# A two-layer attention and expert kernel on one core: experts by halves of the batch, fp32 products in the last network, exps read from PSUM, and a new order of the work

## The chip, the cores and the metric

One core of one Trainium2 chip runs the kernel. The metric is the device time of one execution in microseconds (us). Three runs of the kernel before gave a median of 160.07 us (159.89 to 160.13).

## What is computed

Eight sequences of 128 tokens with 128 features go through four blocks, each added to its own input. Cut to what matters:

```python
x = x + softmax(LN(x) @ ctx.T) @ ctx                      # first attention, 77 context rows per sequence
m = heads(LN(x)) @ o_w + o_b                              # 16 heads over 128 tokens
x = LN(x) + x + 0.3 * sum_e comb[e] * (gelu(m @ w1[e] + b1[e]) @ w2[e] + b2[e])   # 8 experts, 2 weights not zero
Sim = hc @ w1s + (hq @ w2s) + (hc * w3) @ hq.T + b_sim    # hc = LN(x), hq = ctx: second attention
A = softmax(Sim, 2); B = softmax(max(Sim, 2), 1)
hat = A @ hq; bar = B @ hc
x = x + [hc, hat, hc * hat, hc * bar] @ W_qv + b_qv
h = gelu(LN(x) @ W1[7] + b1[7])                           # last network, one expert of hidden size 512
x = x + (h @ W2[7] + b2[7]) * softmax(LN(x) @ Wr.T)[7]
```

The term `hq @ w2s` is one number for each row of the context: the context's row, the same for all tokens.

## The kernel before

**Queues.** The order of the work is one list written out by hand, `plan`. Each engine's program walks it and runs the stages that it owns, so the list fixes the order on PE, ACT, DVE, POOL and SP at once; semaphores join the queues. A stage is named with its arguments: `m1:u,e,c` is the first product of expert e for the tokens of unit u and half c of the hidden features, `gelu:u,e` its two gelus on ACT, `m2:u,e` its second product, `acc:u,e` the weighted adds on DVE. PE never reorders.

**Units.** From the experts on, the batch goes in three units: unit 0 is sequences 0 to 3 (512 tokens), units 1 and 2 are two sequences each (256 tokens). In the kernel before every stage of the experts is done for each unit. `m1` is two products in fp32r (low part of w1 and high part, each against the tokens, line 1098, which is a helper through which nearly all products go), 512 or 256 columns wide; `m2` is in fp32, 128 columns, which the profile shows as two records for each product: 16 records for a unit of four sequences, 8 for a unit of two. `h1_bank` names the PSUM banks of m1: two pairs of banks, taken in turn.

**Second attention** (`p4_*`), for each unit: layer norm (`p4_ln`, the power on POOL at line 571, `p4_norm`), transposes to x3T (`p4_T`), the similarities (`p4_sim`), on DVE an add of `simrow` (line 1006), the maximum and its subtraction (line 1011), one exp over the unit's scores (`p4_exp`, line 727, ACT), the softmax over the tokens through `p4_mx`, `p4_nbm` and `bex` (line 730), the sums and the scaling (`p4_probs`), transposes (`p4_pT`), products with context and tokens (`p4_hq`), `p4_hh` on DVE, the output products (`p4_out`, 3 for each sequence) and `p4_outd` on DVE (line 1048). `simrow` holds the context's row for all sequences; PE makes it in two products 308 wide between the heads (`p4_ctx`, with `w2sq`), ACT copies it (line 718).

**Last network** (`p5_*`): layer norm, transposes (`p5_T`), router (8 columns), `p5_f1:u,c` as three fp32r products (`split3`; ACT makes the high part of the tokens at line 751, DVE the low part at line 1058), a gelu each (line 760), `p5_f2:u,i` in fp32 for each sequence, the last add on DVE (line 1084) and the store. `p5_exp:2`, `p5_prob:2` and `p5_end:2` come after the last gelus.

ACT holds one set of function tables: exp and ln are in one set, gelu in another, and each change of set is an ACT_TABLE_LOAD. `warm` and `hot` are products with no use for the result, which keep PE busy.

## Time and profile before

| what | before |
|---|---|
| median of 3 runs | 160.07 us |
| the profiled execution, its own time | 160.33 us |
| its span on the core | 158.5 us |
| PE busy with products | 146.0 us (92%) |
| PE loading weights | 118.0 us (74%) |
| DVE, ACT, POOL busy | 109.3, 105.9, 50.5 us |
| stages in time | front to 30, heads to 71, experts from 71, second attention and last network among them from 103 |

The span is the time from the first to the last instruction; 1.8 us of the execution lie around it. Busy shares are averages over stages, and the ends of PE's records are modelled: successive products overlap in the record. What a product costs in a stream is the distance from its start to the next start, and a wait of PE is where that distance exceeds the usual one of its kind.

### The profile page before, as it was taken

Reading aid. Unit: us, or ns where it says so; the run is one execution under the profiler, and the core shown is the slowest. Engines: PE = TensorE matmul, PEld = TensorE weight load, DVE = VectorE, ACT = ScalarE, POOL = GpSimd, SP = SyncE. Lnnn points to the kernel's source line nnn. Section 1 sums busy time; section 2 is a strip of 40 time slices with the busy share of each in tenths; the row PEclk is TensorE's granted clock in tenths of the full one; section 3 lists DMA queues with packets and bytes.
Section 4 is the critical chain, followed back from the end, with each engine's and each line's share of the span. In section 5 each row is a group of like instructions: output and inputs, shape, how many; then the busy total and the mean of one; then the engine's idle time right before and its main releaser. Section 6 shows DMA issues by size and latency. Waiting matters only on the chain.

```text
span 158.5 us, 3986 instructions
## 1 busy us (share of the span) xinstructions
PE 146.0 (92%) x1288; PEld 118.0 (74%) x1296; DVE 109.3 (69%) x413; ACT 105.9 (67%) x238; POOL 50.5 (32%) x155
## 2 busy tenths in 40 slices
PE   7898995889999999999999999998999999999891
PEld 5676872555766557567998999997899889779780
DVE  3666999978877749832269656963764968687733
ACT  5697795368388677999489344657941894666480
POOL 7799500234244478594000001400430200400100
PEclk9999999999999999999999999999999999999999
DMA  3528700743557423100100000000000000000022
GB/s 100 156 76 271 203 2 0 149 115 74 113 155 181 104 50 54 19 2 4 35 0 4 0 0 0 4 0 2 0 4 0 2 6 0 0 0 2 4 67 65
DMA packets 11072, 8.03 MB, mean 51 GB/s; under 512 B 1867, under 2 KB 10155, under 8 KB 11051
## 3 DMA queue, kind: packets, MB, share of 16 engines
q1 hardware_dynamic: 11051, 7.76, 19.7%
q8 instruction: 11, 0.18, 0.5%
q14 instruction: 10, 0.08, 0.2%
HBM read 5.26 MB, written 1.70 MB: 44 GB/s over the span
## 4 chain that ended last, share of the span: by engine, by line
PE 49%; issue 21%; DVE 14%; ACT 7%; POOL 4%; DMA 2%; ACTq 1%; SPq 1%; POOLq 1%; DVEq 0%
PE ps L1098 47%; DVE qbd L876 2%; DVE nmax L882 2%; DMA x<-in_x_dram 2%; POOL rstd L571 2%; DVE stats L784 1%; DVE xn L799 1%; ACT pr L631 1%; ACT pexp L662 1%; POOL xn L565 1%; ACTq L58 1%; ACT L727 1%; DVE mv L788 1%; ACT mT L655 1%; DVE res L851 1%
## 5 line engine op out<-in xcount | busy, mean ns | idle before, releaser
L712 ACT ACTIVATE vpad<-ps,b1o 128x256 f32<-128x256 f32 (+1 forms) x48 | 23.3, 543 | 17.3 <-PE ps L1098 17.1
L1098 PE MATMUL ps<-w2s,vpad 128*128 128x128 f32 x256 | 32.4, 276 | 0.0
L1098 PEld LDWEIGHTS ps<-w2s,vpad 128*128 128x128 f32 x256 | 30.4, 192 | 0.8 <-issue 0.2
L995 DVE SCALAR_TENSOR_TENSOR vpad<-ps,comb,vpad 128x128 f32<-128x128 f32 x64 | 18.4, 343 | 10.3 <-PE ps L1098 10.1
L882 DVE TENSOR_REDUCE nmax<-ps 128x4 f32<-128x512 f32 x32 | 20.9, 685 | 5.5 <-PE ps L1098 5.4
L662 ACT ACTIVATE pexp<-ps 128x512 f32<-128x512 f32 x32 | 18.2, 594 | 2.5 <-PE ps L1098 1.9
L1098 PE MATMUL ps<-ao,w_lo 128*128 128x256 f32 (+1 forms) x48 | 16.4, 356 | 0.8 <-ACT vpad L712 0.8
L1098 PE MATMUL ps<-ao,w_hi 128*128 128x256 f32 (+1 forms) x48 | 14.6, 318 | 0.0
L565 POOL TENSOR_TENSOR xn<-vpad,bqv 128x256 f32<-128x256 f32 (+1 forms) x3 | 2.7, 915 | 36.5 <-DVE vpad L995 36.5
L571 POOL TENSOR_TENSOR rstd<-veps,power 128x2 f32<-128x2 f32 (+1 forms) x6 | 4.8, 808 | 28.2 <-DVE veps L794 28.2
L1098 PE MATMUL ps<-kst,qbd 128*128 128x128 bf16 x128 | 11.8, 219 | 2.1 <-DVE nmax L882 2.1
L1098 PEld LDWEIGHTS ps<-kst,qbd 128*128 128x128 bf16 x128 | 8.6, 97 | 6.8 <-issue 5.0
L1098 PE MATMUL ps<-qbd,kst 128*128 128x512 bf16 x32 | 12.1, 383 | 0.9 <-ACT mT L655 0.3
L1098 PE MATMUL ps<-pexp,vpad 128*32 128x128 f32 x256 | 10.8, 280 | 0.2
L1098 PEld LDWEIGHTS ps<-ao,w_lo 128*128 128x128 f32 x48 | 9.1, 189 | 2.5 <-issue 1.8
L1098 PE MATMUL ps<-ones 128*128 128x256 bf16 x46 | 9.3, 336 | 1.1 <-DVE pair L775 1.1
L1098 PEld LDWEIGHTS ps<-ao,w_hi 128*128 128x128 f32 x48 | 9.1, 189 | 0.4
L556 POOL COPY qbd<-mT 3x256 f32<-3x256 f32 x16 | 6.6, 414 | 7.7 <-ACT mT L655 7.3
L760 ACT ACTIVATE qbd<-ps,cols 128x256 f32<-128x256 f32 (+1 forms) x12 | 6.3, 544 | 3.8 <-PE ps L1098 3.7
L1098 PEld LDWEIGHTS ps<-pexp,vpad 128*32 128x32 f32 x256 | 5.9, 108 | 3.5 <-issue 1.3
L1098 PE MATMUL ps<-f2s,qbd 128*128 128x128 f32 x64 | 8.3, 278 | 0.0
L541 POOL CAST xn<-nmax 128x16 bf16<-128x16 f32 x8 | 2.0, 255 | 19.0 <-DVE nmax L882 18.9
(228 smaller groups left out, 331.2 us busy)
## 6 DMA issues: line engine op xcount, KB each, us to landing
w1s<-in_L_ffn_w_dram SPq DMA_DIRECT2D x1, 1024.0 KB, 5.4
kst<-scratch_k SPq DMA_DIRECT2D x8, 72.0 KB
qbd<-scratch_q SPq DMA_DIRECT2D x8, 72.0 KB
w1s<-w1s SPq DMA_DIRECT2D x8, 64.0 KB
x<-in_x_dram SPq DMA_DIRECT2D x2, 192.0 KB, 3.6
scratch_q<-part SPq DMA_DIRECT2D x2, 144.0 KB, 2.6
scratch_k<-part SPq DMA_DIRECT2D x2, 144.0 KB, 2.5
wqv<-in_L_xattn_W_qv_dram SPq DMA_DIRECT2D x1, 256.0 KB, 3.2
```

The lines of the kernel that those rows point to most:

```text
L58: with stack:
L541: a = did(pool.tensor_copy(m[:, :, 0, :], v))
L556: last = pool.tensor_copy(qbd[r, g, :, b * S:(b + 1) * S].bitcast(FP32), mT[r, b % 2, :, :].bitcast(FP32))
L565: pool.tensor_tensor(out=x2b[:, seqs(u), :], in0=x2[:, seqs(u), :], in1=bqv[:, :].unsqueeze(1).to_broadcast([P, UNITS[u][1], D]), op=ALU.a ...
L571: pool.tensor_tensor(out=rstd[:, i, seqs(u)], in0=veps[:, i, seqs(u)], in1=power[:, seqs(u)], op=ALU.pow).then_inc(s[f"ln{i}_rstd"], 1)
L662: act.activation(pexp[:, n % 3, :], ps[:, 2 + n % 2, :], ACT.Exp, scale=KPH ** -0.5).then_inc(s["p_ok"], 1)
L712: act.activation(hT[:, k % 2, c, 0:n], ps[:, h1_bank(k, c), 0:n], ACT.Gelu, bias=b1o[:, e, c:c + 1]).then_inc(s["gelu_ok"], 1)
L760: act.activation(gT[:, c, toks(u)], ps[:, (bank_a, bank_b)[c % 2][u], 0:UNITS[u][1] * S], ACT.Gelu, bias=cols[:, R_FB1 + c:R_FB1 + c + 1]) ...
L876: last = dve.tensor_scalar(out=qbd[r, g, j, 0:FRONT[0][1] * S], in0=kst[r, g, T // 2:T], scalar1=used1[r, 0:1], scalar2=None, op0=ALU.mult)
L882: dve.tensor_reduce(nmax[:, b, g, :], ps[:, n % 2, :].rearrange("p (j t) -> p j t", t=S), axis=AX.X, op=ALU.max, negate=True).then_inc(s[" ...
L995: dve.scalar_tensor_tensor(out=x2[:, a + i, :], in0=ps[:, 2 + k % 2, i * D:(i + 1) * D], scalar=comb[:, a + i, e:e + 1], in1=x2[:, a + i, ...
L1098: return nc.tensor.matmul(dst, lhsT, rhs, start=start, stop=stop)
```

## The change

Five parts. (1) `m1` and `gelu` run for two halves of the batch instead of three units: half 1 holds units 1 and 2, all products are 512 wide; the gelus of half 1 go to a buffer of their own for all eight experts (`hT1`, in the room of the dead `qbd`), so they wait for no `m2`; `m2` and `acc` stay by units. The last network's gelus move to other dead tiles. (2) `p5_f1` of units 1 and 2 is one fp32 product instead of three fp32r ones; ACT's copy of the high part and DVE's subtraction fall away there. (3) The context's row is added by PE in `p4_sim` itself, as a product that accumulates in the same bank; `p4_ctx`, `simrow` and the add on DVE go. DVE takes the negated maximum from PSUM; the exps are taken from PSUM for each sequence with that maximum as bias and an accumulated sum (2 or 4 instead of 1), so DVE's subtraction and sum go too; a small DVE operation makes `nmb`, from which the softmax over the tokens is made. (4) In `p4_out` of units 1 and 2 the two products that don't need `hh` come first, each sequence in a bank of its own. (5) The whole `plan` is in a new order. There are 43 `warm` products instead of 44 and one `hot` instead of two; before the first transposes of the context stand 12 `warm` instead of 20. By SP's queue nothing changes: the same transfers in the same order. On ACT the changes of table fall from ten to eight after the first load: `p4_exp:0` and `p4_exp:1` now stand with no gelu between them.

The diff, cut to its core (of the plan: the front's part that the text speaks of, and everything from `p4_T:0` on):

```diff
-            p1_soft:1 p1_pT:1 warm:2 p1_ln:0 warm:1 z_den warm:1 spare warm:1 p1_norm1:0 setup p1_av:1 a_q:2 p1_T2:0 p1_T:2 warm:1
...
-            av:6,3 s2:7,2 av:7,0 fb s2:7,3 p4_ctx:1 norm:5 den:6 av:7,1 av:7,2 un:7 x2_init:0 norm:6 av:7,3 cT:0 den:7 m1:0,0,0
...
-            m1:1,4,0 m1:1,4,1 x2b:1 m1:1,5,0 m1:1,5,1 m2:1,3 acc:1,2 p4_T:0 m2:1,4 gelu:1,5 p4_norm:0 gelu:1,6 p4_sim:0 m1:1,6,0
-            m1:1,6,1 m1:1,7,0 acc:1,3 m2:1,5 m1:1,7,1 m1:2,0,0 acc:1,4 m2:1,6 p4_simd:0 m1:2,0,1 acc:1,5 gelu:1,7 m1:2,1,0 acc:1,6
-            p4_mx:0 m2:1,7 p4_nbm:0 gelu:2,0 p4_exp:0 gelu:2,1 p4_probs:0 m2:2,0 m1:2,1,1 acc:1,7 p4_pT:0 gelu:2,2 m1:2,2,0
-            m1:2,2,1 acc:2,0 fw1 p4_ln:1 m2:2,1 p4_hq:0 p4_norm:1 m1:2,3,0 m1:2,3,1 m2:2,2 p4_hh:0 acc:2,1 m1:2,4,0 m1:2,4,1
-            gelu:2,3 acc:2,2 gelu:2,4 p4_outd:0 gelu:2,5 p4_T:1 p5_ln:0 acc:2,3 p4_out:0 m2:2,3 m1:2,5,0 acc:2,4 gelu:2,6
-            p4_simd:1 m1:2,5,1 m2:2,4 acc:2,5 p4_exp:1 gelu:2,7 p4_nbm:1 p5_norm:0 m1:2,6,0 m1:2,6,1 p4_sim:1 m2:2,5 p4_probs:1
-            p4_mx:1 m1:2,7,0 m1:2,7,1 p5_T:0 m2:2,6 acc:2,6 acc:2,7 p4_pT:1 m2:2,7 p5_router:0 p4_hh:1 p4_ln:2 p4_hq:1 p5_f1:0,0
-            p4_norm:2 p5_f1:0,1 p4_outd:1 p4_out:1 p5_f1:0,2 p4_T:2 p5_ln:1 p5_f1:0,3 p4_sim:2 p4_simd:2 x2b:2 p5_norm:1 p5_exp:0
-            p4_nbm:2 p5_f2:0,0 p4_mx:2 p4_exp:2 p4_probs:2 p5_f2:0,1 p5_prob:0 p4_pT:2 p5_T:1 p4_hq:2 p4_hh:2 p5_f2:0,2
-            p5_router:1 p4_outd:2 p5_exp:1 p4_out:2 p5_f1:1,0 p5_ln:2 p5_norm:2 p5_f1:1,1 p5_f2:0,3 p5_f1:1,2 p5_f1:1,3 p5_T:2
-            p5_prob:1 p5_f2:1,0 p5_router:2 p5_end:0 p5_end:1 p5_f1:2,0 p5_prob:2 p5_f1:2,1 p5_f1:2,2 p5_f1:2,3 p5_f2:1,1
-            p5_f2:2,0 p5_f2:2,1 p5_end:2 p5_exp:2
...
+            p1_pT:1 warm:4 p1_ln:0 a_q:1 warm:1 spare p1_norm1:0 warm:2 p1_av:1 setup p1_T2:0 oT warm:2 p1_qk:0 p1_ln:1 p1_split:0
...
+            norm:5 av:7,1 av:7,2 s2:7,3 den:6 norm:6 av:7,3 un:7 cT:0 den:7 norm:7 m1:0,0,0 x2_init:0 gelu:0,0 b2:0 gelu:0,1
...
+            gelu:1,4 acc:1,3 gelu:1,5 p4_T:0 m1:1,5,1 m1:1,6,0 acc:1,4 m1:1,6,1 m2:1,3 m2:1,4 gelu:1,6 m1:1,7,0 gelu:1,7 x2b:0
+            m1:1,7,1 m2:1,5 p4_sim:0 m2:1,6 p4_mx:0 m2:1,7 p4_exp:0 acc:1,5 p4_simd:0 m2:2,0 acc:1,6 p4_pT:0 p4_nbm:0 p4_probs:0
+            x2b:1 acc:1,7 p4_hq:0 m2:2,1 m2:2,2 acc:2,0 da:1 p4_hh:0 acc:2,1 p4_ln:1 acc:2,2 p4_norm:1 p4_out:0 p4_outd:0 p4_T:1
+            p5_ln:0 acc:2,3 p4_simd:1 x2b:2 m2:2,3 p5_norm:0 p4_exp:1 p4_sim:1 acc:2,4 acc:2,5 p4_nbm:1 m2:2,4 p4_probs:1 p4_mx:1
+            acc:2,6 m2:2,5 acc:2,7 p5_T:0 m2:2,6 m2:2,7 p4_pT:1 p5_router:0 p4_hq:1 p4_hh:1 p5_f1:0,0 p5_f1:0,1 p4_out:1 p4_ln:2
+            p5_f1:0,2 p4_norm:2 p4_T:2 p5_f1:0,3 p4_exp:2 p4_sim:2 p4_mx:2 p4_outd:1 p5_ln:1 p5_f2:0,0 p4_simd:2 p4_nbm:2
+            p5_norm:1 p5_f2:0,1 p4_pT:2 p5_exp:0 p5_T:1 p4_hq:2 p4_probs:2 p4_hh:2 p5_router:1 p5_exp:1 p4_outd:2 p5_ln:2
+            p5_f2:0,2 p4_out:2 p5_f1:1,0 p5_f1:1,1 p5_f1:1,2 p5_f1:1,3 p5_f2:0,3 p5_norm:2 p5_T:2 p5_f2:1,0 p5_prob:0 p5_router:2
+            p5_f1:2,0 p5_f1:2,1 p5_prob:1 p5_f1:2,2 p5_end:0 p5_end:1 p5_f1:2,3 p5_prob:2 p5_end:2 p5_f2:1,1 p5_f2:2,0 p5_exp:2
+            p5_f2:2,1
...
                 for c in range(F0):
                     act.wait_ge(s["h1_ps"], F0 * k + c + 1)
-                    if k >= 2:
+                    if u == 0 and k >= 2:
                         act.wait_ge(s["h2_ps"], k - 1)
                     if k == 0:
                         act.wait_ge(s["b1o_ok"], 1)
-                    act.activation(hT[:, k % 2, c, 0:n], ps[:, h1_bank(k, c), 0:n], ACT.Gelu,
+                    act.activation(hT1[:, e, c, :] if u else hT[:, k % 2, c, :], ps[:, h1_bank(k, c), :], ACT.Gelu,
                                    bias=b1o[:, e, c:c + 1]).then_inc(s["gelu_ok"], 1)
-
...
+                    act.activation(pr[1][:, b, :], ps[:, bank_b[u], m * CTX:(m + 1) * CTX], ACT.Exp, bias=mx[1][:, b:b + 1],
+                                   accum_out=rs[1][:, b:b + 1]).then_inc(s["pr1_ok"], 1)
                 act.wait_ge(s["nbm_ok"], u + 1)
-                act.activation(bex[0:n, u, :], ps[0:n, bank_b[u], 0:S], ACT.Exp, bias=nbm[0:n, u:u + 1],
+                act.activation(bex[0:n, u, :], ps[0:n, bank_a[u], 0:S], ACT.Exp, bias=nbm[0:n, u:u + 1], scale=-1.0,
                                accum_out=bsum[0:n, u:u + 1]).then_inc(s["bex_ok"], 1)
 
...
                 dve.wait_ge(s["sim_ps"], u + 1)
-                dve.wait_ge(s["sr_ok"], NHALF)
-                dve.tensor_tensor(out=sc[1][:, us, :], in0=ps[:, bank_b[u], 0:n * CTX].rearrange("p (b c) -> p b c", c=CTX),
-                                  in1=simrow[:, us, :], op=ALU.add).then_inc(s["sc1_ok"], 1)
-                dve.wait_ge(s["sc1_ok"], u + 1)
-                a = did(dve.tensor_reduce(mx[1][:, us], sc[1][:, us, :], axis=AX.X, op=ALU.max))
-                after(a)
-                dve.tensor_tensor(out=sc[1][:, us, :], in0=sc[1][:, us, :], in1=wide(mx[1][:, us])(CTX),
-                                  op=ALU.subtract).then_inc(s["sim_sub"], 1)
+                dve.tensor_reduce(mx[1][:, us], ps[:, bank_b[u], 0:n * CTX].rearrange("p (b c) -> p b c", c=CTX), axis=AX.X,
+                                  op=ALU.max, negate=True).then_inc(s["sim_max"], 1)
+                dve.wait_ge(s["sim_max"], u + 1)
...
-                    pe.wait_ge(s["gelu_ok"], F0 * (k - (2 if k <= 2 * E0 else 1)) + c + 1)
+                    pe.wait_ge(s["gelu_ok"], F0 * (k - 2) + c + 1)
                 f = slice(c * P, (c + 1) * P)
-                dst, x = ps[:, h1_bank(k, c), 0:n], ao2[:, :, :].rearrange("p h t -> p (h t)")[:, toks(u)]
+                dst, x = ps[:, h1_bank(k, c), :], ao2[:, u, :]
                 mm(dst, w1_lo[:, e, f], x, True, False)
...
+                pe.wait_ge(s["w2sq_ok"], 1)
+                pe.wait_ge(s["ctxT_ok"], NFRONT)
+                mm(ps[:, bank_b[u], 0:n * CTX], w2sq[:, :], ctxT[:, seqs(u), :].rearrange("p b c -> p (b c)"), True, False)
                 pe.wait_ge(s["xT2_ok"], u + 1)
                 pe.wait_ge(s["ctxw_ok"], NHALF)
                 for m in range(n):
-                    last = mm(ps[:, bank_b[u], m * CTX:(m + 1) * CTX], x3T[:, toks(u, m)], ctxw[:, a + m, :])
+                    last = mm(ps[:, bank_b[u], m * CTX:(m + 1) * CTX], x3T[:, toks(u, m)], ctxw[:, a + m, :], False, m == n - 1)
...
+                pe.wait_ge(s["w14_ok"], u + 1)
+                if u:
+                    for m in range(UNITS[u][1]):
+                        p4_two(u, m)
                 pe.wait_ge(s["hh_ok"], u + 1)
-                pe.wait_ge(s["w14_ok"], u + 1)
-                for m in range(n):
-                    dst = ps[:, bank_b[u], m * D:(m + 1) * D]
-                    mm(dst, hqT[:, toks(u, m)], wqv[:, 1, :], True, False)
-                    mm(dst, hhT[:, toks(u, m)], wqv[:, 2, :], False, False)
-                    last = mm(dst, x3T[:, toks(u, m)], w14[:, a + m, :], False, True)
+                for m in range(UNITS[u][1]):
+                    if u == 0:
+                        p4_two(u, m)
+                    last = mm(p4_bank(u, m), hhT[:, toks(u, m)], wqv[:, 2, :], False, True)
                 last.then_inc(s["qv_ps"], 1)
...
+                    pe.wait_ge(s["l7_sub"] if c else s["xT3_ok"] if u else s["x4hi_ok"], u + 1)
                 f = slice(c * P, (c + 1) * P)
-                split3(ps[:, (bank_a, bank_b)[c % 2][u], 0:UNITS[u][1] * S], f1_hi[:, f], f1_lo[:, f],
-                       x4_hi[:, toks(u)], x4_lo[:, toks(u)]).then_inc(s["f1_ps"], 1)
+                dst = ps[:, (bank_a, bank_b)[c % 2][u], 0:UNITS[u][1] * S]
+                if u == 0:
+                    last = split3(dst, f1_hi[:, f], f1_lo[:, f], x4_hi[:, toks(u)], x4_lo[:, toks(u)])
+                else:
+                    last = mm(dst, f1s[:, f], x4T[:, toks(u)])
+                last.then_inc(s["f1_ps"], 1)
 
...
```

## Rows read from the trace of the kernel before

**Rows 1.** Windows: length; busy us of PE, PEld, DVE, ACT, POOL; PEclk, DMA share, GB/s.
```profile
14.96:30.49 15.53, 12.78 (x92) 9.07 (x90) 15.01 (x53) 10.36 (x26) 4.29 (x11) 1.00 0.37 95
30.49:70.95 40.46, 38.74 (x493) 24.90 (x501) 29.98 (x86) 31.17 (x74) 21.93 (x76) 1.00 0.40 90
70.95:103.16 32.21, 32.21 (x247) 29.70 (x247) 19.62 (x87) 20.22 (x35) 4.57 (x6) 1.00 0.03 6
103.16:152.18 49.02, 46.85 (x362) 42.31 (x361) 34.25 (x138) 31.56 (x71) 7.02 (x9) 1.00 0.01 2
152.18:158.50 6.32, 2.84 (x26) 2.65 (x24) 2.07 (x8) 1.97 (x3) 0.00 (x0) 1.00 0.29 83
```

**Rows 2.** Timeline of PE, m1 512 wide: start us, us, then the instruction.
```profile
84.37 0.39 PE L1098 MATMUL ps<-ao,w_hi 128*128 128x512 f32 x1
...
87.40 0.43 PE L1098 MATMUL ps<-ao,w_lo 128*128 128x512 f32 x1
```

**Rows 3.** Timeline of PE, m1 256 wide, then m2 of 16 records.
```profile
98.52 0.37 PE L1098 MATMUL ps<-ao,w_lo 128*128 128x256 f32 x1
98.72 0.28 PE L1098 MATMUL ps<-ao,w_hi 128*128 128x256 f32 x1
...
99.54 1.95 PE L1098 MATMUL ps<-w2s,vpad 128*128 128x128 f32 x16
101.24 0.37 PE L1098 MATMUL ps<-ao,w_lo 128*128 128x256 f32 x1
```

**Rows 4.** Timeline of PE, f1 of unit 1 as three products.
```profile
144.97 0.36 PE L1098 MATMUL ps<-ao_hi,f_lo 128*128 128x256 f32 x1
...
145.76 1.05 PE L1098 MATMUL ps<-f2s,qbd 128*128 128x128 f32 x8
```

**Rows 5.** Timeline of PE, an fp32 product 512 wide (two records).
```profile
24.33 1.10 PE L1098 MATMUL ps<-w1s,woT 128*128 128x512 f32 x2 [0.33 <-ACT w1s L694]
25.27 0.49 PE L1161 MATMUL ps<-ident,pr 128*77 128x128 f32 x3
```

**Rows 6.** Timeline of PE, the second p4_ctx product and what follows it.
```profile
68.61 0.68 PE L1098 MATMUL ps<-ctxT,w2sq 128*128 128x308 f32 x2
69.13 0.38 PE L1098 MATMUL ps<-un,selden 128*128 128x128 f32 x2
```

**Rows 7.** Groups by line and shape: busy us, mean ns, idle before and releaser.
```profile
L712 ACT ACTIVATE vpad<-ps,b1o 128x256 f32<-128x256 f32 x32 | 13.4, 471 | 11.0 <-PE ps L1098 10.9
L712 ACT ACTIVATE vpad<-ps,b1o 128x512 f32<-128x512 f32 x16 | 9.9, 687 | 6.3 <-PE ps L1098 6.2
L718 ACT ACTIVATE simrow<-ps,bsim 128x308 f32<-128x308 f32 x2 | 1.0, 518 | 0.0
```

**Rows 8.** Timeline of ACT, a change of table and the exp behind it.
```profile
109.52 1.28 ACT L727 ACT_TABLE_LOAD   x1
110.81 0.46 ACT L727 ACTIVATE pr<-sc 128x308 f32<-128x308 f32 x1
```

**Rows 9.** Timeline of PE, a wait behind that stretch of ACT.
```profile
108.53 0.28 PE L1098 MATMUL ps<-ao,w_hi 128*128 128x256 f32 x1
109.28 0.36 PE L1098 MATMUL ps<-ao,w_lo 128*128 128x256 f32 x1 [0.48 <-ACT vpad L712]
```

**Rows 10.** Timeline of DVE, the add and the subtraction around the maximum of unit 0.
```profile
105.60 0.48 DVE L1006 TENSOR_TENSOR sc<-ps,simrow 128x308 f32<-128x308 f32 x1 [0.30 <-PE ps L1098]
...
106.62 0.48 DVE L1011 TENSOR_TENSOR sc<-sc,mx 128x308 f32<-128x308 f32 x1
```

**Rows 11.** Chain of waits: three exps with accumulated sums, first attention.
```profile
11.21 1.00 ACT pr L631 x6
```

**Rows 12.** Timelines of DVE and POOL behind p4_out of unit 0.
```profile
121.99 0.69 DVE L1048 TENSOR_TENSOR vpad<-ps,xn 128x512 f32<-128x512 f32 x1 [2.21 <-PE ps L1098]
...
124.28 1.01 POOL L571 TENSOR_TENSOR rstd<-veps,power 128x4 f32<-128x4 f32 x1 [7.84 <-DVE veps L794]
```

**Rows 13.** Timeline of PE in the front, the output products of the first attention.
```profile
13.99 0.94 PE L1098 MATMUL ps<-ctxn,pT 77*128 77x128 f32 x6
```

136 lines of the change are left out of this document (73 added, 63 removed).

## The prediction, made before the changed kernel ran

> **What bounds the kernel now.** I read the windows first, cut where the work changes: front, heads, first experts, everything from the first transposes of the second attention (`p4_T:0`, 103.16), and the end from the last f1 product (152.18) [rows 1]. The reader is to see that three regimes follow each other. From 14.96 to 30.49 DVE is busy 15.0 of 15.5 us: the front is DVE's. From 30.49 to 70.95 PE is busy 38.7 of 40.5 us. From 70.95 to 103.16 it is busy all the time: there only PE's own work counts. From 103.16 to 152.18 it shows 46.9 of 49.0, and DVE and ACT have room. The granted clock is 1.00 (2.4 GHz) in all of them. Next I read PE's timeline by distances from start to start, since the records overlap. m1 512 wide: thirteen steps from 84.37 to 87.40, 0.233 each [rows 2]. m1 256 wide: the first product behind another kind takes 0.20, the next seven fill 98.72 to 99.54, 0.117 each; m2's 16 records take 1.70, with their entry about 1.78, so 8 records 0.85 to 0.89 [rows 3]. With such prices the stretch from 103.16 to 152.18 holds 44.0 us of products: 12 m2 10.7, 20 m1 pairs 256 wide 5.7, `p4_out` 5.3, f1 6.5, five f2 4.5, sim, hq, transposes, routers and the rest 11.3. So **5.0 us of its 49.0 are waits of PE**, more than the busy share lets one think. Such a wait is the one behind ACT at 108.53 to 109.28: 0.75 from start to start where 0.12 is usual [rows 9].
>
> **The change part by part.**
>
> *Halves of the experts.* 64 products 256 wide (64 x 0.117 = 7.5, and some 16 entries of 0.08 more, 8.8) become 32 of 512 wide (32 x 0.233 = 7.5, some 7 entries, 8.0): 0.8 off PE. Twice the columns cost twice the time, so only entries are saved. On ACT a whole batch half is 32 gelus 256 wide or 16 gelus 512 wide: 13.4 busy against 9.9 [rows 7], 3.5 off, and nothing waits for it where PE is full. But the work moves: up to `p4_T:0` PE now runs 11 pairs 512 wide (5.5) where it ran 12 pairs 256 wide and one more m2 (3.2 + 0.9), so **the stretch from 70.95 gets 1.4 longer**, and the one after it loses 20 pairs (5.7), gains 5 (2.5) and that m2: 2.3 less.
>
> *fp32 in f1.* Three products in a stream are 0.40, half of the 0.79 that six take [rows 4]. An fp32 product 512 wide takes 0.94 [rows 5], half as wide 0.47: 8 x 0.07 = 0.6 more, 0.2 once the entries it saves are taken off. DVE and ACT lose about 0.4 each for two units; the last router no longer stands behind the subtraction. I take +0.2 in PE's work; bounds 0 and +0.6.
>
> *The context's row.* 0.52 for a product 308 wide [rows 6]; the two in the heads go (1.04), and 0.52 + 0.26 + 0.26 come into the later stretch. DVE's add and subtraction of 0.48 [rows 10] go: `p4_sim` to the exps is 1.0 shorter for unit 0, some 0.65 for the small ones. The exps get longer: three with sums took 1.00 [rows 11], so four take 1.3 and two 0.7 instead of 0.46 [rows 8] and about 0.3. Net 0.2 to 0.3 off the chain of each unit.
>
> *Tables.* In the row the exp starts 1.29 after the table's start [rows 8]: a change costs ACT 1.29, two fewer give 2.6. The Trainium skill, page "ScalarE: Activation LUTs", section "What ACT_TABLE_LOAD costs", counts 2.66 us for a change, as a drain follows the load. By it two changes fewer would give ACT 5.3; the row shows no such drain, so I stay with 1.29, and the rule is the ground of the third rival.
>
> *Heads and front.* `hot` once less, 0.1. Without `p4_ctx:1` the last exp of the heads has only `den:6` beside it: `av:7,3` waits for an exp (308 wide it is 0.46 [rows 8]) and its latency, with less than 0.3 of cover; I take 0.5 for that wait, between 0 and 0.8. So the heads get 1.04 + 0.1 - 0.5 = 0.65 shorter. In the front `p1_av:1`, which started at 13.99 [rows 13], behind the columns' transposes, now goes before them, about 0.7 earlier; DVE, which is full after it [rows 1], starts earlier but also meets ACT's fills before `rows:0`; I take 0.3 of the 0.7. The rest of the new order in front and heads can't be read from rows: PE is idle for 1.7 us in the heads and 2.7 in the front [rows 1], and the order may give back or cost 1.0. I take nothing, and keep -1.0 and +1.0.
>
> *The long stretch.* I went through the new list from `p4_T:0` (time 0), each stage at its price, each wait by its releaser:
> - PE's fillers (T, three m1, two m2, two m1, m2) and the row with sim:0 reach 7.0; maximum 0.5, four exps 1.3, bex and scaling 1.1 end at 9.8, PE comes to pT:0 at 10.0: covered. hq:0 ends at 12.4, two m2 14.2, out:0 16.9.
> - Behind out:0 DVE has the add and the statistics, 2.3 from 121.99 to POOL's start [rows 12], the acc of m2:2,3 and the maximum: 20.4. PE stands at mx:1 from 19.6: **wait 0.8**. Then m2:2,5, p5_T:0 (POOL's 1.0 is just covered), two m2, pT:1, router, hq:1: 26.2; two f1 27.6; out:1 29.0.
> - f1, T:2, f1, sim:2: 31.4. mx:2 waits 0.6. Two f2: 34.1. The gelu-to-exp change on ACT ends at 32.8, so pT:2 is just ready; hq:2 waits 0.3, out:2 ends at 38.5, four f1 (0.3 of waits), f2, T:2, f2 and the router at 42.8, the last f1 at 45.0.
>
> That is 45.0 against 49.0, with 2.1 us of waits instead of 5.0. What went: the m1 that waited for gelus behind the tables, of which one is shown [rows 9], and the waits before mx:1, pT:1 and T:2. What is late next is DVE behind out:0. Such a walk finds no collisions of two late queues; where half of the 2.9 us of recovered waits come back, the stretch is at 46.5. **I take 46.0, 3.0 less.** The end, 6.3 us from there [rows 1], is the same chain: gelu, table, exp, router's probabilities, add.
>
> **Sum:** front -0.3, heads -0.65, first experts +1.4, long stretch -3.0, order elsewhere 0: -2.55. The profiled execution's own time, 160.33 (span 158.5 and 1.8 around it), becomes 157.8; the median of the runs stands 0.26 below that execution, so I forecast **157.5**. A measurement can tell some 0.2% from no change, 0.3 us here.
>
> **The rivals.**
>
> *Only the work goes (chance 0.19).* PE's own work falls by 0.8 (m1) + 0.1 (hot) - 0.2 (f1), 0.7; if other waits take the place of the old, the time falls by 0.3 to 1.7: 158.4 to 159.8. For it: DVE is the late one in my walk already. Against it: DVE and ACT lose work in that very stretch.
>
> *The order is better everywhere (0.15).* If the walk holds in full (-4.0) and the order of heads and front gives back 1 of their 4.4 us of waits, it is -0.3 - 0.65 + 1.4 - 4.0 - 1.0 = -4.55, with more up to -6: 154 to 156. For it: ACT loses 3.5 of gelus, 2.6 of tables and the 1.0 of `simrow` [rows 7]. The rule of the Trainium skill on table changes (the page named above) points this way, but more strongly: with 1.4 more for each of the two changes that go, ACT would give back 2.8 more. As rows have it, PE waited 0.63 behind one such place [rows 9]; two places with 1.3 each would be the most, inside this rival.
>
> *Slower: the second attention runs out of cover (0.10).* Before, 20 m1 pairs (5.7 us) stood between the links of the chain norm, transposes, scores, exps, transposes, products, norm of units 0 and 1. Now only m2 stand there. If that chain and not PE sets the stretch, it stays at 49.0 or grows by the longer exps (0.9) while the first experts are 1.4 longer and heads and front 0.95 shorter: 160.1 + 0.5 to + 1.4, 160.6 to 161.5. It decides from 48.6 us of stretch. Against it: in the rows unit 0 needs 5.2 from the scores' add (105.60) to the exp (110.81) only since gelus and a table stood before it [rows 8, 10].
>
> *The front loses its clock or its DVE time (0.02).* All stretches show the granted clock at 1.00 [rows 1], but with 12 instead of 20 products before the first transposes PE does less there. At half the clock for some microseconds, or with DVE later, the price is an estimated 1 to 3.5: up to 161.
>
> *The change does nothing that counts (0.04):* within 0.3 of 160.07.
>
> **How the numbers follow.** The forecast's own case, -1.7 to -4.0, has 0.50: 156.1 to 158.4. Faster by over 0.2%: 0.50 + 0.19 + 0.15 = 0.84; within 0.2%: 0.05 with the edge of the slower case; slower: 0.11. The range: 156.1 to 158.4 holds 0.50; up to 159.8 takes in the second case; down to 155.3 takes half of the third (the walk in full, -4.55, is 155.5). Together about 0.78.
>
> **What would show it.** In the changed kernel: m1 starts 0.233 apart and 32 such products only; `p4_T:0` about 0.4 later than 103.16 (102 to 104); from it to the last f1 45 to 47; the first wait of PE there before the small `nmb` product of unit 1; nine tables in all; ACT's exps 0.33 apart; `av:7,3` behind the last exp. Wrong would be a stretch of 48.6 or more, a wait over 1 us before pT:0 or T:0 of the last network, DVE later than 15 in the front, or f1 fp32 products over 0.55 each.

## The result: 0.66% faster, where 1.6% was forecast

The changed kernel took 160.06 us (median of 20 runs, 158.73 to 161.16), the kernel before 160.91 in the 20 runs beside it (159.86 to 162.63). The medians differ by 0.85 us. The ratio, which leaves out the few runs that are far above the fastest of their kernel, is 0.9934, 95% interval 0.9908 to 0.9959, which of 160.91 is 1.06 us less. The sign was right; the forecast was 2.6 us less and 157.5, and the measured time lies outside the range. Part of the distance is the base: with the later runs the kernel before lies 0.8 above the 160.07 of its first three. Both kernels have runs in which TensorE is granted half its clock for some 3.4 us, and these take about 1 us more (e1 and e17 below). The runs of the changed kernel with a mean clock of 0.995 or more have a median of 159.2 (20 of the 32 taken, e3 included), those of the kernel before 160.3 (47 of the 122 with a clock on record). With the low clock it is 160.3 against 161.4. So the change is worth 1.1 us either way, over all runs; the two kernels with the fill of e1 and e2 differ by less, 0.6.

The page of the changed kernel, its span, its PE line and the granted clock in 40 slices:

```profile
span 158.2 us, 3846 instructions
PE 146.2 (92%) x1256; PEld 116.2 (73%) x1256; DVE 107.6 (68%) x405; ACT 100.7 (64%) x229; POOL 50.6 (32%) x155
PEclk9999999699999999999999999999999999999999
```

PE (TensorE) is as busy as it was; part of this execution ran at half the clock, and with the clock even (e1 and e2) it is 146.6 against 147.2. The windows of the changed kernel, cut at the same places as [rows 1] (`fold:0`, the first m1, `p4_T:0`, the last block of f2; columns as there):

```profile
22.62:71.15 48.53, 45.31 (x528) 27.59 (x528) 36.68 (x108) 33.44 (x82) 21.27 (x78) 0.96 0.36 83
71.15:104.80 33.65, 33.65 (x236) 30.11 (x236) 20.51 (x83) 22.64 (x36) 8.00 (x11) 1.00 0.02 5
104.80:151.84 47.04, 45.07 (x338) 40.57 (x337) 31.95 (x132) 24.69 (x63) 5.65 (x7) 1.00 0.01 2
151.84:158.20 6.36, 2.84 (x25) 2.65 (x23) 2.52 (x10) 1.97 (x3) 0.00 (x0) 1.00 0.31 85
```

Read against [rows 1]: the first experts 32.21 to 33.65, so 1.44 longer; the long stretch 49.02 to 47.04, 1.98 shorter; the end 6.32 to 6.36. The heads show a mean clock of 0.96, so this profile can't say what they gained; e1 and e2 can.

Waits of PE in the long stretch, timeline of the changed kernel (all with an idle time of 0.2 or more):

```profile
125.53 0.38 PE L1097 MATMUL ps<-ident,nmb 128*2 128x128 f32 x2 [0.60 <-DVE nmb L1011]
137.79 0.38 PE L1097 MATMUL ps<-ident,nmb 128*2 128x128 f32 x2 [0.68 <-DVE nmb L1011]
145.79 1.10 PE L1097 MATMUL ps<-xT,f1s 128*128 128x256 f32 x4 [0.23 <-ACT w1s L762]
150.01 1.10 PE L1097 MATMUL ps<-xT,f1s 128*128 128x256 f32 x4 [0.24 <-DVE lg L935]
151.34 0.67 PE L1097 MATMUL ps<-xT,f1s 128*128 128x256 f32 x2 [0.23 <-ACT w1s L762]
```

The first is where the prediction put it, before unit 1's `nmb` product (it transposes the negated maxima, stage `p4_mx`); no m1 waits for a gelu any more (the wait of [rows 9] is gone). From start to start the last three cost about 0.4 each.

Where in the stretch the 2.0 us were gained is read from products that stand in both kernels: `p4_mx:1`, the f1 product behind `p4_out:1`, the one behind `p4_out:2`, and the last block of f2. In the kernel before, the first two are

```profile
126.22 0.38 PE L1098 MATMUL ps<-ident,mx 128*2 128x128 f32 x2 [0.20 <-DVE sc L1011]
...
135.09 0.48 PE L1098 MATMUL ps<-ao_hi,f_lo 128*128 128x512 f32 x1
```

and the third is the first line of [rows 4]. In the changed kernel the second and third are

```profile
134.45 0.48 PE L1097 MATMUL ps<-ao_hi,f_lo 128*128 128x512 f32 x1
...
144.53 1.03 PE L1097 MATMUL ps<-xT,f1s 128*128 128x256 f32 x4
```

| from `p4_T:0` to | before | changed | gain | the walk |
|---|---|---|---|---|
| `p4_mx:1` | 23.1 | 20.7 | 2.3 | 20.4 |
| out:1 done | 31.9 | 29.65 | 2.3 | 29.0 |
| out:2 done | 41.8 | 39.7 | 2.1 | 38.5 |
| last f1 done | 49.0 | 47.0 | 2.0 | 45.0 |

The last column is the prediction's walk through the new list. The whole gain is there at `p4_mx:1`; behind it the kernel before takes 26.0, the changed one 26.3, and the walk had 24.6. PE's work behind it is nearly the same in both: the changed kernel has one m2 and one row product more (0.9 and 0.3) and four m1 products fewer (0.8).

### The profile page after: what moved, and what is told of

It reads as the page before. It is cut to its first block, busy times and chain, and to the rows that moved or that the text cites. A ratio compares the mean times of both kernels' runs of the same rounds, so it can differ in the third digit from the quotient of the medians.

```text
span 158.2 us, 3846 instructions
## 1 busy us (share of the span) xinstructions
PE 146.2 (92%) x1256; PEld 116.2 (73%) x1256; DVE 107.6 (68%) x405; ACT 100.7 (64%) x229; POOL 50.6 (32%) x155
## 4 chain that ended last, share of the span: by engine, by line
issue 42%; PE 24%; POOL 12%; DVE 11%; ACT 5%; DMA 2%; ACTq 1%; POOLq 1%; SPq 1%; DVEq 0%
PE ps L1097 22%; POOL w_lo L527 3%; DVE qbd L878 2%; DVE nmax L884 2%; DMA x<-in_x_dram 2%; POOL rstd L575 2%; POOL xn L569 2%; POOL w_hi L525 2%; ACT pexp L666 1%; PE ps L1137 1%; DVE xn L1072 1%; ACTq L58 1%; POOL f_lo L534 1%; DVE res L853 1%; DVE stats L786 1%
## 5 line engine op out<-in xcount | busy, mean ns | idle before, releaser
L1097 PE MATMUL ps<-w2s,qbd 128*128 128x128 f32 x128 | 16.4, 278 | 0.0
L1097 PEld LDWEIGHTS ps<-w2s,qbd 128*128 128x128 f32 x128 | 15.4, 192 | 1.0 <-issue 0.6
L1097 PEld LDWEIGHTS ps<-w2s,vpad 128*128 128x128 f32 x128 | 15.0, 192 | 0.7 <-ACT vpad L716 0.2
L1097 PE MATMUL ps<-w2s,vpad 128*128 128x128 f32 x128 | 15.4, 276 | 0.0
L716 ACT ACTIVATE qbd<-ps,b1o 128x512 f32<-128x512 f32 x16 | 9.9, 698 | 7.1 <-PE ps L1097 7.1
L1097 PE MATMUL ps<-ao,w_lo 128*128 128x512 f32 x32 | 13.5, 421 | 0.0
L716 ACT ACTIVATE vpad<-ps,b1o 128x512 f32<-128x512 f32 x16 | 9.9, 687 | 4.5 <-PE ps L1097 4.5
L1097 PE MATMUL ps<-ao,w_hi 128*128 128x512 f32 x32 | 12.6, 395 | 0.0
L1097 PE MATMUL ps<-ones 128*128 128x256 bf16 x44 | 8.6, 330 | 1.1 <-DVE pair L777 1.1
L1097 PEld LDWEIGHTS ps<-ao,w_lo 128*128 128x128 f32 x32 | 6.0, 189 | 1.5 <-issue 0.2
```

Source lines behind the costliest of these rows:

```text
L716: act.activation(hT1[:, e, c, :] if u else hT[:, k % 2, c, :], ps[:, h1_bank(k, c), :], ACT.Gelu, bias=b1o[:, e, c:c + 1]).then_inc(s["gel ...
L1097: return nc.tensor.matmul(dst, lhsT, rhs, start=start, stop=stop)
```

## The experiments

Stage lengths below come from profiles, from the start of one named product to the start of another; in the later stretches they repeat within 0.04 from profile to profile, while the total moves by 0.5 and more. The front's start jitters by 0.8 (the first transposes at 5.75 to 6.57 over all profiles), the rest of the front and the heads by some 0.3. The experiments ran in groups on different chips, so medians of different groups compare only roughly; a ratio is to the kernel before in its own group.

### e1, e2, e3: the low clock

```diff
+            def fill(n):
+                pe.wait_ge(s["ones_ok"], 1)
+                pe.wait_ge(s["kq_ok"], 3)
+                for _ in range(n):
+                    keep_clock(7)
...
-            ... p1_pT:2 s1:0,2 ...
+            ... p1_pT:2 fill:12 s1:0,2 ...
```

> The changed kernel with 12 more products 256 wide between p1_pT:2 and s1:0,2, where PE stood idle for 1.32 us before 27.22. In its profile the granted clock then was 0.50 from about 28.9 to 32.3; its 20 runs fall in two groups, 158.7 to 159.5 and 160.0 to 160.9, and the lower one has a clock of 0.995 or more. Theory A (the idle stretch before brings the low clock): the filled kernel has a clock of at least 0.99 in nearly every run and about 158.9 us in all, 1.2 less than the upper group. Theory B (the low clock comes from something that the idle stretch does not decide): two groups again, 158.9 and 160.1. Theory C (the fill holds up s1:0,2 or the clock is lost elsewhere): 159.3 or more in every run.

> The kernel before with the same 12 products at the same place, where PE stood idle for 1.64 us before 27.39. Its runs lay in two groups as well, 159.9 to 160.2 and 161.4 to 162.6. Theory A: one group at 160.0. Theory B: two groups as before. If the whole difference of the two kernels is outside of the clock, this kernel stays 1.1 to 1.5 us above the changed one with the same fill.

> The changed kernel itself, beside the other two on the same chip, for the share of runs with a low clock. Both theories: 158.9 where the clock is 1.00, 160.1 where it is 0.989; against the kernel before 0.993.

Measured: e1 159.48 (159.12 to 160.55, ratio 0.9935, 0.9907 to 0.9963), e2 160.08 (159.74 to 160.61, ratio 0.9952, 0.9925 to 0.9979), e3 160.16 (159.00 to 161.53, ratio 0.9942, 0.9901 to 0.9982). Of the 24 runs of e1 and e2 none had a clock under 0.995; of the 12 of e3 four had 0.986 to 0.989. The end of the gap in the changed kernel's timeline of PE, then in e3's:

```profile
27.22 0.38 PE L1097 MATMUL ps<-kst,qbd 128*128 128x128 bf16 x4 [1.32 <-DVE nmax L884]
```

```profile
27.18 0.38 PE L1097 MATMUL ps<-kst,qbd 128*128 128x128 bf16 x4 [1.33 <-DVE nmax L884]
```

Windows of the changed kernel:

```profile
28.00:29.00 1.00, 1.00 (x11) 1.00 (x9) 0.94 (x3) 0.00 (x0) 0.00 (x0) 0.94 0.96 194
29.00:32.00 3.00, 3.00 (x15) 1.72 (x15) 2.66 (x13) 1.33 (x4) 1.18 (x6) 0.50 0.57 122
32.00:33.00 1.00, 1.00 (x3) 0.31 (x3) 1.00 (x4) 0.14 (x1) 0.74 (x3) 0.85 0.12 24
```

and with the fill (e1):

```profile
29.00:32.00 3.00, 2.49 (x18) 1.23 (x17) 2.96 (x15) 1.75 (x5) 1.54 (x6) 1.00 0.52 108
```

The PEclk column falls to 0.50, the lower level of 1.2 GHz, from just before 29 to just after 32. The same work then takes PE longer: s2:0,0 starts 4.11 after `fold:2` and 3.13 in e1. What came before is PE's idle time of 1.32 that ends at 27.22. Theory A holds: with products in that gap the clock stayed up, in all but 2 of the 114 timed runs of the twelve filled kernels that were run more than once. The gap by itself doesn't decide it: e3's profile has the same gap and a clock of 1.00 throughout. As the kernel before falls into it at least as often (75 of 122 runs against 12 of 32; in the group of e3, 13 of 29 against 4 of 12), it isn't the change's doing. The fill gives nothing where the clock holds by itself: its stages from `fold:0` to s2:0,0 take 9.29, e3's 9.30. e1's median is 0.2 above that of the eight runs of e3 at full clock (159.25), which is within their spread.

A part of e2's expectation missed: it was to stay 1.1 to 1.5 above e1 and stays 0.6 above (160.08 against 159.48). Why that is half of the 1.1 without the fill is not settled; both kernels' totals move by 0.5 and more.

All later kernels but e17 have the fill, and are compared with e1 or e2. Windows of e1, then of e2:

```profile
22.34:70.28 47.94, 45.27 (x541) 27.88 (x540) 36.59 (x108) 33.57 (x82) 21.23 (x78) 1.00 0.36 84
70.28:103.91 33.63, 33.63 (x236) 30.11 (x236) 20.50 (x83) 22.60 (x36) 8.00 (x11) 1.00 0.02 6
103.91:150.94 47.03, 45.06 (x339) 40.58 (x338) 31.98 (x132) 24.66 (x63) 5.65 (x7) 1.00 0.00 1
```

```profile
21.94:70.47 48.53, 45.89 (x545) 28.85 (x545) 37.73 (x109) 35.26 (x85) 22.98 (x81) 1.00 0.37 83
70.47:102.69 32.22, 32.22 (x246) 29.70 (x246) 19.64 (x87) 20.25 (x35) 4.59 (x6) 1.00 0.03 6
102.69:151.72 49.03, 46.85 (x362) 42.31 (x361) 34.25 (x138) 31.59 (x71) 7.03 (x9) 1.00 0.01 2
```

The change at full clock, stage by stage: heads -0.59, first experts +1.41, long stretch -2.00, and the front longer by 0.1 to 0.4 (22.34 against 21.94 here, 22.62 against 22.48 without the fill). The spans differ by 0.8, the medians of e1 and e2 by 0.6.

### e3 and e11, e17: a late copy in SP's queue

e3's profile has the clock at 1.00 throughout and is still 1.0 longer than e1's. SP's queue and ACT in e1:

```profile
50.39 4.61 SPq L422 DMA_DIRECT2D w1s<-w1s  x4
55.04 2.52 SPq L428 DMA_DIRECT2D aoT<-aoT  x4
...
59.25 0.75 ACT L686 ACTIVATE ao_hi<-aoT,signs 128x512 fp32r<-128x512 f32 x1
```

and in e3:

```profile
50.53 6.03 SPq L422 DMA_DIRECT2D w1s<-w1s  x4
56.60 2.49 SPq L428 DMA_DIRECT2D aoT<-aoT  x4
...
60.47 0.72 ACT L686 ACTIVATE ao_hi<-aoT,signs 128x512 fp32r<-128x512 f32 x1 [1.18 <-DMA aoT<-aoT]
```

The copy of the tokens (`da:0`) stands behind the doubling of w1 (`dw:0`), whose last issue waits for the landings of those before it. In e3 it went out 1.56 later, and ACT stood 1.18 at the high part of the tokens (`ao_hi`) with the exps of the heads behind it. The three profiles with the longest waits of this kind (e3, e16 and e7: 1.18, 1.06, 0.53, with 6.03 to 6.09 for the four issues) also have the longest heads: 48.73 in e3 and e16, where the other profiles of the new order at full clock and without the row products have 47.6 to 48.1; and 49.07 in e7, where e2 has 48.53. e11 moves five later loads (wqv, bqv, f1s, f2s, fb2s, at the end of `parts`), 2.4 us of issues that stood ahead of both, behind that copy:

```diff
-                sp.dma_start(wqv[:, :, :], ...)
...
+            def late():
+                sp.dma_start(wqv[:, :, :], ...)
...
-            ... da:0 ...
+            ... da:0 late ...
```

> The changed kernel (fill of e1) with the five loads of the last weights (wqv, bqv, f1s, f2s, fb2s: 2.4 us of SP's queue from 47.1 to 49.5) moved behind the first copy of the tokens (da:0). In e3, with the clock at 1.00, that copy was issued at 56.60 instead of 55.04, since the doubling of w1 in front of it took 6.03 us instead of 4.61, and the first high part on ACT came 1.2 late, the end 1.0 late. Theory T (SP's queue ahead of da:0 makes the runs of 160.0 and more at full clock): the runs lie closer together, median 158.9 to 159.2, the highest under 159.7. Theory U (the late issue is covered in most runs, other waits make the spread): the same spread as e1, 159.1 to 160.5, median 159.4.

> The changed kernel with the late loads of e11 but without the fill. Theory A of e1 (the low clock is brought by the idle stretch before s1:0,2): part of the runs have a clock of 0.989 and are 1.0 to 1.3 above the others, which lie at 158.7 to 159.2; no run at full clock is above 159.7. If the fill did nothing, the runs look like those of e11, 159.0 to 159.7.

Measured: e11 159.16 (six runs, 158.97 to 159.70; ratio 0.9885, 0.9844 to 0.9927). e17, without the fill: 158.89, 158.94 and 159.17 at a clock of 0.997 and more, 159.85, 159.90 and 159.93 at 0.989 (ratio 0.9889, 0.9850 to 0.9928). In e11 the doubling is issued from 48.14 on, is through at 52.2, and the copy goes out at 55.04, when its input is ready. In the five profiles with the late loads (e11, e14, e15, e17, e18) the four issues take 4.05 or 4.06, in those without 4.61 to 6.09. So two causes of spread are apart: the clock gave 0.9 us in half of e17's runs, and the queue made e3's profile 1 us long at full clock. Theory A holds once more. Theory T holds for e11 and e17, but not to the letter and not for every run: e11's highest is 159.70, and one run of e18, which has the late loads, stands 1.6 above its kernel's median at full clock (162.10), with no profile of it. e11 is the lowest of the kernels so far: 0.3 below e1 by medians, from another group; the intervals of the two ratios overlap.

### e4, e5: fp32 in f1

e4 puts the three fp32r products, ACT's high part and DVE's low part back for units 1 and 2; e5 takes them out of the kernel before.

```diff
-                if u == 0:
-                    last = split3(dst, ...)
-                else:
-                    last = mm(dst, f1s[:, f], x4T[:, toks(u)])
+                last = split3(dst, ...)
```

> The changed kernel (with the fill of e1, whose stretch from p4_T:0 to the last block of f2 products is 47.03 us) with f1 of units 1 and 2 as three fp32r products again, and with ACT's high part and DVE's subtraction for them. Theory P (in this stretch PE's own work sets the time, and fp32 in f1 was underpriced by some 0.8): the stretch falls by 0.5 to 0.9, to 46.1 to 46.5. Theory Q (from p4_out:1 on it is the chain through DVE, POOL and ACT, and PE's products fill its gaps): the stretch stays within 0.2 of 47.0 or grows by up to 0.4, since the last router then stands behind the subtraction.

> The kernel before (with the fill of e2, stretch 49.03) with f1 of units 1 and 2 as one fp32 product each, nothing else changed. Theory P: the stretch grows by 0.5 to 0.9. Theory Q: within 0.2, or shorter by up to 0.4 (the last router no longer waits for the subtraction).

Measured: e4 159.38, stretch 47.12 (e1 47.03); e5 160.54, stretch 49.36 (e2 49.03). In the new order this part is worth nothing either way, -0.09; in the old one it costs 0.33. Two fp32 products with their entry fill 145.79 to 146.73 of the changed kernel, 0.47 each as forecast, 0.07 above the 0.40 of the split [rows 4]. Theory Q for e4; e5 lies between the two.

### e6, e7: the context's row and the exps

e6 is the changed kernel with `simrow`, `p4_ctx`, add, subtraction and one exp as before, in the new order; e7 the kernel before with this part alone, in the old order.

```diff
-                a, n = UNITS[u]
-                for m in range(n):
-                    act.activation(pr[1][:, b, :], ps[...], ACT.Exp, bias=mx[1][:, b:b + 1], accum_out=...)
+                act.activation(pr[1][:, seqs(u), :], sc[1][:, seqs(u), :], ACT.Exp)
...
-            ... un:5 mT:7 ... s2:7,3 den:6 ...
+            ... un:5 p4_ctx:0 mT:7 ... s2:7,3 p4_ctx:1 den:6 ...
```

> The changed kernel (with the fill of e1) with the context's row made once between the heads again (two products 308 wide, a copy by ACT), added on DVE, the maximum subtracted on DVE and one exp for a unit. The prediction had 1.04 for the two products in the heads, so these should grow by 1.0 or, where they hide in waits, by less. Theory P for the long stretch: PE loses the three row products (1.09 in its records), so the stretch falls by 0.5 to 1.0. Theory Q: it grows, since each unit's chain from the scores to the maximum's transposes gets an add and a subtraction (0.5 each for unit 0, 0.3 for the small ones) and the exps start later: by 0.4 to 1.2, to 47.4 to 48.2.

> The kernel before (with the fill of e2: first m1 at 70.47, stretch 49.03) with the context's row added by TensorE, the exps from PSUM and no other part of the change, in the old order. The first m1 should come up to 1.0 earlier. Theory P: the long stretch grows by 0.5 to 1.0 (three row products more on PE). Theory Q: it falls by 0.4 to 1.2 (shorter chains of units 1 and 2), and this part alone would carry a good part of the 2.0 by which the whole change shortens it.

Measured: e6 160.48 (160.24 to 160.60 but for one run; ratio 0.9950, 0.9911 to 0.9989), heads 48.35 (e1 47.94), stretch 47.91, 0.88 longer. e7 161.74 (161.12 to 163.14; ratio 1.0045, 1.0003 to 1.0088), stretch 50.68, 1.65 **longer** (its profile's heads, 49.07, hold a late copy of the tokens as e3's do: 6.08 for the four issues). So the same part takes 0.88 off the stretch in the new order and adds 1.65 in the old one, more than either theory had for e7. The part is three things at once (row products on PE, no add and subtraction on DVE, exps by sequence on ACT); none of them was tried alone. What the timelines of ACT and PE show, of e2:

```profile
110.35 0.46 ACT L727 ACTIVATE pr<-sc 128x308 f32<-128x308 f32 x1
110.72 0.34 ACT L730 ACTIVATE bex<-ps,nbm 4x128 f32<-4x128 f32 x1
```

and of e7:

```profile
111.84 0.33 ACT L723 ACTIVATE pr<-ps,mx 128x77 f32<-128x77 f32 x1
112.06 0.19 ACT L723 ACTIVATION_READ_ACCUMULATOR pr<-ps,mx 128x1 f32 x1
...
113.05 0.34 ACT L726 ACTIVATE bex<-ps,nbm 4x128 f32<-4x128 f32 x1
...
114.04 0.38 PE L1089 MATMUL ps<-ident,batt 4*128 4x4 f32 x2 [0.73 <-DVE batt L1020]
```

From the first exp to `bex` it is 0.37 in e2 and 1.21 in e7: four exps, each with a read of its sum (0.30 a pair). In the old order ACT is the late one there (gelus of unit 1 and a table load stand before), PE waits 0.73 behind it, and unit 0's transposes start 10.32 after `p4_T:0` instead of 9.06: 1.26 of the 1.65. Of this the exps are 0.84. The rest stands before them: the row product goes ahead of m1 on PE, the next m1 starts 0.46 later (2.66 after `p4_T:0` against 2.20), and so does the table load behind its gelus. The other 0.39 comes with units 1 and 2, each with a row product more. In the new order ACT has its table loaded and waits for the maximum (0.68 in the changed kernel), and m2 products run on PE until after the exps (its transposes come 10.13 after `p4_T:0` in e1, 10.34 in e6). There DVE's add and subtraction are what is felt: in e6 PE waits before `p4_mx:1`

```profile
125.91 0.38 PE L1106 MATMUL ps<-ident,mx 128*2 128x128 f32 x2 [1.30 <-DVE sc L1017]
```

where it waits 0.60 in e1, and the product comes 0.64 later after `p4_T:0`.

Everything else of the change, without this part (e6 against e2), takes 1.12 off the stretch and adds 1.33 to the first experts; the median is 0.4 above e2, while the ratios to the kernel before are alike (0.9950 and 0.9952). Neither half of the change is shown to be faster than e2 alone; together they are.

### e9, e10: the order of front and heads

e9 is the kernel before with the new order up to the first m1, e10 the changed kernel with the old one up to there.

```diff
-            a_v:0 warm:3 z_sel:0 ... den:7 norm:7 m1:0,0,0 ...
+            warm:8 a_q:0 warm:5 ... den:7 norm:7 m1:0,0,0 ...
```

> The kernel before (fill of e2: fold:0 at 21.94, first m1 at 70.47) with the changed kernel's order up to the first m1, the two context row products put in at the corresponding places, and the old order from there. The prediction gave the order nothing in front and heads beside 0.3 of the front. Theory R (the heads' gain of 0.6 to 1.0 in the changed kernel comes from the row products that left): here front and heads together stay within 0.3 of the kernel before, and the front is 0.1 to 0.4 longer. Theory S (the new order itself gives it): the first m1 comes 0.5 or more earlier though the row products are there.

> The changed kernel (fill of e1: first m1 at 70.28) with the old order of front and heads, without the row products. Theory R: first m1 at 69.3 to 70.0, as early as in e1 or earlier. Theory S: at 70.8 or later. The stretches behind it stay at 33.63 and 47.03 in both.

Measured: e9 160.36 (ratio 0.9969, 0.9936 to 1.0003), heads 48.60 (e2 48.53), first m1 at 70.97. e10 159.76 (ratio 0.9920, 0.9886 to 0.9954), heads 48.07 (e1 47.94), first m1 at 70.25. This is theory R in the main, though e10's first m1 lies between the two ranges named: in the old order the row products that left give 0.46 (48.53 to 48.07); the new order gives 0.13 more or, with the products there, nothing, which is within the spread. In the front it gives nothing: `fold:0` starts at 22.18 in e10 and 22.37 in e9. Counted from the first transposes, which takes the jitter of the start out, `fold:0` comes 15.99 to 16.36 later in the five profiles of the old order and 16.18 to 16.95 in those of the new one.

### e13: the width of m1

```diff
-                mm(dst, w1_lo[:, e, f], x, True, False)
-                mm(dst, w1_hi[:, e, f], x, False, True).then_inc(s["h1_ps"], 1)
+                for v in (whole,) if u == 0 else (first_half, second_half):
+                    mm(dst[:, v], w1_lo[:, e, f], x[:, v], True, False)
+                    last = mm(dst[:, v], w1_hi[:, e, f], x[:, v], False, True)
+                last.then_inc(s["h1_ps"], 1)
```

> The changed kernel (fill of e1: first m1 to p4_T:0 33.63, from there 47.03) with each m1 product of the second half as two 256 wide ones, unit by unit, the gelus as they are. The prediction took 0.8 off PE for the wider products, from entries saved. If it is the number of products that costs, the first of the two stretches grows by 0.5 or so (11 of the 16 pairs lie there); if only a change of kind costs (an entry each time another kind of product has run), both stretches stay within 0.15.

Measured in one run: 159.56; first experts 33.65 (33.63), long stretch 47.06 (47.03). 32 more products cost 0.05. So a product costs its columns here, and the number of products is not what the halves can save; that they save changes of kind, as the prediction had it, was not measured by itself.

### e8, e12, e16: what bounds the long stretch

The first edit is e8's, the second (for u == 2, e >= 4 alone) e12's, and e16 has both. These kernels leave out part of the result: half of the second products' sum, or all but one column of the adds, for four experts and unit 2. Each was run once.

```diff
-                    for c in range(F0):
+                    for c in (range(1) if u == 2 and e >= 4 else range(F0)):
...
-                    dve.scalar_tensor_tensor(out=x2[:, a + i, :], ...
+                    dve.scalar_tensor_tensor(out=x2[:, a + i, 0:1], ...
```

> The changed kernel (fill of e1, long stretch 47.03) with the second products of experts 4 to 7 for unit 2 summed over one half of the hidden features only, so 16 of their 32 records, about 1.8 us of PE's work, fall away between the scores of unit 1 and the first f1; nothing else waits for less. This leaves out part of the result on purpose of the measurement: the weights' other half for these experts and tokens. Theory P (PE's own work sets the stretch): it falls by 1.5 to 1.8, to about 45.3. Theory Q (the chain of units 1 and 2 through DVE, ACT and POOL sets it): it falls by under 0.6, and the freed time shows as waits of PE before pT:1 and the transposes.

> The counterpart of e8: the changed kernel (fill of e1, long stretch 47.03) where the 8 weighted adds on DVE of experts 4 to 7 for unit 2 run over one column of 128 instead of all, about 0.2 less each, 1.5 us of DVE's work in all. This leaves out that part of the result. Theory D (between the scores of unit 1 and the transposes of unit 2 the bound is DVE, full from 120.5 to 133): the stretch falls by 0.7 to 1.5. Theory P (PE's own work): under 0.3. Theory H (neither engine's work but the hops between engines): under 0.3 as well, with idle time on both.

> The edits of e8 and e12 together (16 records less on PE, 8 adds cut to one column on DVE, part of the result left out), on the changed kernel with the fill (long stretch 47.03; 46.67 in e8, 46.84 in e12). Theory J (PE and DVE are both close to full there, so that taking work from one only shows the other): the stretch falls by clearly more than the sum of the two, 0.55, namely by 1.2 or more, to 45.8 or less. Theory H (hops and other links set it, whatever the two engines have to do): by 0.3 to 0.6.

Windows of the stretch, of e8:

```profile
104.12:150.79 46.67, 43.59 (x322) 38.90 (x321) 31.84 (x132) 24.68 (x63) 5.66 (x7) 1.00 0.00 1
```

of e12:

```profile
103.93:150.77 46.84, 44.88 (x338) 40.56 (x337) 31.09 (x132) 24.67 (x63) 5.65 (x7) 1.00 0.00 1
```

and of e16, in three parts:

```profile
104.90:128.60 23.70, 22.39 (x176) 20.43 (x174) 15.95 (x66) 10.22 (x30) 2.45 (x3) 1.00 0.01 1
128.60:137.00 8.40, 8.38 (x47) 7.50 (x48) 5.72 (x25) 4.99 (x10) 1.81 (x2) 0.80 0.01 2
137.00:152.60 15.60, 14.24 (x101) 12.11 (x100) 9.41 (x42) 9.60 (x25) 1.39 (x2) 1.00 0.00 1
```

e8 takes 16 records and 1.47 of busy time off PE, and the stretch falls by 0.36; the rest shows as waits:

```profile
124.84 0.38 PE L1097 MATMUL ps<-ident,nmb 128*2 128x128 f32 x2 [1.05 <-DVE nmb L1011]
126.71 1.20 PE L1097 MATMUL ps<-w2s,qbd 128*128 128x128 f32 x8 [0.28 <-DVE vpad L997]
128.30 0.38 PE L1097 MATMUL ps<-ident,batt 2*128 2x2 f32 x2 [0.39 <-DVE batt L1026]
```

e12 takes 0.9 of busy time off DVE (1.5 was expected) and gives 0.19. So neither PE's load nor DVE's alone sets the stretch: theory P is out for this part of it, and D as far as 0.9 tells. With both (e16) the first f1 comes 26.01 after `p4_T:0` instead of 26.84: 0.83 earlier, more than the 0.55 of the two and less than J's 1.2. Behind it e16 says nothing: the granted clock fell (0.80 in the mean from 128.60 to 137.00), and the stretch ended at 47.7. Before it PE had waits of 1.04 and 0.27; but e8, with the waits above, kept 1.00, so that the missing work brought the low clock is not shown.

### e14, e15, e18: the order of the links

e14 makes unit 0's f1 fp32 as well; e15 moves two stages on DVE; e18 lets PE's order follow. All three start from e11. The first edit of the plan is in e15 and e18, the second in e18.

```diff
-            ... p5_ln:0 acc:2,3 p4_simd:1 x2b:2 m2:2,3 p5_norm:0 ... acc:2,5 p4_nbm:1 m2:2,4 ...
+            ... p5_ln:0 p4_simd:1 acc:2,3 x2b:2 m2:2,3 p4_nbm:1 p5_norm:0 ... acc:2,5 m2:2,4 ...
...
-            ... p5_T:0 m2:2,6 m2:2,7 p4_pT:1 p5_router:0 p4_hq:1 p4_hh:1 p5_f1:0,0 p5_f1:0,1 p4_out:1 ...
+            ... p5_T:0 p4_pT:1 m2:2,6 m2:2,7 p4_hq:1 p5_router:0 p4_hh:1 p5_f1:0,0 p4_out:1 p5_f1:0,1 ...
```

> The kernel of e11 (fill, late loads; long stretch 47.03, median 159.16) with f1 of unit 0 as fp32 products too, so that DVE's subtraction (0.67, at 129.26), ACT's high part (0.57) and POOL's splitting of the weights fall away; PE gets 4 products of two records instead of 12 of one. Theory D: the transposes of unit 2 come 0.4 to 0.7 earlier and the stretch is 0.2 to 0.6 shorter. Theory P: the stretch is 0.2 to 0.5 longer, as the four products take 3.5 instead of 3.1. Theory H: within 0.2.

> The kernel of e11 with two moves in DVE's order only: the maximum of unit 1's scores ahead of an add of the experts (acc:2,3, 0.53), and the maximum over the tokens (nbm:1) ahead of the norm for the last network's unit 0, behind which it stood ready for some 1.8 us. No work is taken away. Theory D: the total changes by under 0.3, since DVE has the same work in that time. Theory H (the hops of unit 1's chain): the wait of 0.60 before the small product of unit 1 goes and the stretch falls by 0.4 or more.

> The kernel of e15 (fill, late loads, the two moves on DVE; stretch 47.05, where the wait before the small product of unit 1 had gone and the transposes of unit 1 still started at the same place, 24.56 after p4_T:0, since two m2 stood in front of them on PE although their input was ready 1.5 earlier). Now PE's order follows: these transposes ahead of m2:2,6 and m2:2,7, the products behind them ahead of the router, and out:1 ahead of the second f1. No work is taken away. If the order of the two queues against each other is what holds the stretch (Theory O), out:1 comes 0.6 or more earlier and the stretch falls by 0.3 to 0.8, median 158.3 to 158.8. If the chain of unit 2 behind the last add of the experts is the bound (Theory H), out:1 comes earlier but the stretch stays within 0.2 of 47.05.

Measured: e14 159.44 (ratio 0.9916, 0.9890 to 0.9943), stretch 47.47, 0.44 longer: with the subtraction gone from DVE, the four longer products put out:1 0.33 and the transposes of unit 2 0.42 later. e15 159.07 (158.79 to 159.32; ratio 0.9887, 0.9861 to 0.9913), stretch 47.05: unit 1's `nmb` product comes 0.52 earlier and nothing behind it does (theory D's outcome, the total within 0.3). So the wait of 0.60 before it, which the walk had as 0.8, costs nothing where it stands. e18 160.53 (160.18 to 162.72; ratio 0.9947, 0.9911 to 0.9983), stretch 48.47, 1.42 longer. Its waits of PE:

```profile
127.38 0.38 PE L1105 MATMUL ps<-ident,batt 2*128 2x2 f32 x2 [1.05 <-DVE batt L1034]
132.95 0.46 PE L1105 MATMUL ps<-wqv,qk 128*128 128x128 f32 x2 [0.54 <-DVE xn L1044]
```

The transposes of unit 1, put first, hold PE up for 1.05 with two ready m2 behind them, and out:1 for 0.54 with an f1 behind it. Neither theory foresaw this: the m2 that stood ahead were the cover, not the obstacle.

## Why the forecast was wrong, step by step

- **First experts, +1.4:** measured +1.44. That 11 pairs 512 wide replace 12 pairs 256 wide and one m2 was all there was to it.
- **Heads, -0.65:** measured -0.59 at full clock, in one pair of profiles with some 0.3 of jitter. The row products were the source (-0.46 in the old order, e10), and PE does wait for the last exp before `av:7,3`, 0.47 in the changed kernel's timeline.
- **Front, -0.3:** measured +0.1 to +0.4. `p1_av:1` does start 0.7 earlier (13.28 against 13.99), but the transposes behind it do not (14.85 against 14.76), and `fold:0` comes no earlier. That step of 0.4 to 0.7 failed: being earlier on PE was not handed on.
- **Tables:** nine, 1.28 each in the groups of the changed kernel, as taken from [rows 8]. The Trainium skill's page "ScalarE: Activation LUTs", section "What ACT_TABLE_LOAD costs", gives a change 2.66 us, of which 1.28 is the load and the rest a drain. The load is as measured here; no drain is seen, as the exp starts 1.29 after the load does [rows 8], and the load 0.01 after the gelu's end.
- **fp32 in f1, +0.2 (0 to 0.6):** +0.33 in the old order, -0.09 in the new. The three waits in the last f1 products, 1.2 from start to start, were underpriced: the walk had the last four at 2.2, they took 2.75. The kernel before needs 7.2 from `p4_out:2` to there, the changed one 7.3, the walk had 6.5.
- **The context's row, 0.2 to 0.3 off each unit's chain:** 0.88 for the three in the new order, as forecast in size. What was not said is that the saving hangs on the order: three sums took 1.00 [rows 11], so the price of the exps was nearly right (0.30 each instead of 0.33), but it was netted against DVE's without asking whether ACT or DVE is late, and the row products' own price on PE. In e7 the part costs 1.65.
- **The halves, 0.8 off PE:** this was sized on work of PE, and no run takes it by itself. e8 shows that 1.5 of such work, taken out behind `p4_sim:1`, is worth 0.36.
- **The long stretch, -3.0:** measured -1.98. This is the term that failed, 1.0 of the 1.5 to 1.8 by which sum and stages differ; the rest is the front. The failed step is that waits of PE behind `p4_mx:1` would be recovered. Up to there the walk was right (20.4, measured 20.7, before 23.1); from there it had 24.6, where the changed kernel takes 26.3, no less than the 26.0 of the kernel before. Each link is 0.3 to 0.6 late, and no single wait explains it. By the prediction's prices PE's work in the stretch falls by 1.1 (2.3 less, the row products' 1.0 and f1's 0.2 more), so of the measured 2.0 only 0.9 are waits that went, where the walk let them fall by 2.9, from 5.0 to 2.1. That an engine was taken as free when the list said so is the likely reason, not a measured one. The prediction's own rule, half of the 2.9 recovered waits given back, made 46.5, 0.5 short of the 47.0; it then took 46.0 without a reason.

The time fell where the rival "only the work goes" had put it (0.3 to 1.7 less, by 0.7 less of PE's work; the stages give 0.8 to 1.1 less). Its idea that other waits take the place of the old fits what stands behind `p4_mx:1`, but e8, where taking work off PE gives a quarter of it, and e6, where DVE's chain gives 0.88, show that the stretch does not simply follow PE's work. That the total landed there is in part luck. The slower rival, the second attention out of cover, did not come: the stretch was 47.0, its point 48.6. It has its truth in e7 and e18, where a chain with ready work behind it costs 1.4 to 1.7. The rival of the low clock was seen, at 0.50 from 29 to 32, but it is in both kernels, and takes nothing from the difference.

What stays open: what exactly sets the 47.0, as e16 was disturbed, and whether an order exists that takes more; the split of the 1.12 between halves, new order and the banks of `p4_out`, none of which was tried by itself; and which of the three things in the row's part gives the 0.88.

## What to carry to other kernels

Price an edit in the order in which it will run: the same edit (row product, exps by sequence, no add and subtraction) gained 0.9 in one order and lost 1.65 in the other. In a hand walk through queues near their load, each link can come out later than its price, here 2.0 in 45 over three units, so of the 4 us that this walk recovered half came. Compare a walk with the kernel before at several marks and not only at the end: here 1.4 of its 4 us were promised behind `p4_mx:1`, and none of them came. Before dividing a difference of 1 us among reasons, look for what moves the time from run to run by as much: here a low clock behind a gap of 1.3 us on PE, and one late issue in SP's queue.

## What was not expected of the hardware

The granted clock fell to 0.50 for some 3.4 us behind an idle stretch of 1.3 us of PE in the profile of the changed kernel, and not in e3's with the same gap. A mean clock under 0.995 came in 12 of its 32 runs and in 75 of 122 of the kernel before; where the clock fell in those without a profile is not on record. With 12 products in the gap it stayed up but for 2 of 114 runs. It fell for about as long in e16's only run, elsewhere. Four issues on SP's queue, the last of which waits for landings, took 4.61 to 6.09 us in different profiles, and 4.05 or 4.06 in the five with the late loads.
